# Softmax denominators by three groups a half instead of four, with two accumulating transfers

## The reference

```python
x = x + tanh(g_xattn) * xattn(LN(x), ctx, ctx, 16)      # 16 heads of 32
x = x + tanh(g_ffn) * ffn(LN(x), w_gate, w_up, w_down)  # 512 -> 1536 -> 512

# xattn: rotary q and k, then per head
scores = q @ k.T * scale + slope * (key - query)
attn = softmax(scores, axis=-1)
out = attn @ v

# ffn: 4-bit blockwise weights, 16-bit quantization of x, up, gate, gate * sig, gate * up
```

## Time and profile before

| | |
|---|---|
| median of 3 executions | 1968.52 us (1967.97 to 1970.09) |
| the profiled execution | 1968.86 us, span 1967.1 us |
| PE busy in the span | 1738.3 us (88%) |
| DVE, ACT, POOL busy | 1484.7, 1187.7, 898.7 us |
| a half of the attention | 29.2 to 31.9 us |

### The profile page before, as it was taken

How to read it: one execution, slowest core, us unless ns; L and a number is a source line. 1 busy time by engine, 2 the same in 40 slices (tenths; PEclk the granted TensorE clock), 3 DMA queues, 4 the chain that set the end, 5 groups by cost and what they waited for, 6 DMA issues and landing times. The chain is left out here.

```text
span 1967.1 us, 26173 instructions
## 1 busy us (share of the span) xinstructions
PE 1738.3 (88%) x9360; PEld 662.5 (34%) x9360; DVE 1484.7 (75%) x2117; ACT 1187.7 (60%) x1911; POOL 898.7 (46%) x411
## 2 busy tenths in 40 slices
PE   1899999999999999999986999999999910299999
PEld 0222333323333323333223554544444400044444
DVE  6899888888787787887845665648999999855442
ACT  2476776777777777666651232228997678854441
POOL 3499999989999999998630010110000000000000
PEclk9999999999999999999997999999999965599999
DMA  4332233112332222221024565547885357755542
GB/s 113 88 115 81 77 87 87 48 49 57 87 88 55 59 61 82 76 56 25 20 97 133 179 204 201 185 153 245 261 269 194 131 178 248 236 186 170 177 161 75
DMA packets 170914, 250.45 MB, mean 127 GB/s; under 512 B 30272, under 2 KB 101312, under 8 KB 170272
## 3 DMA queue, kind: packets, MB, share of 16 engines
q1 hardware_dynamic: 170784, 248.78, 40.2%
HBM read 146.74 MB, written 76.68 MB: 114 GB/s over the span
## 5 line engine op out<-in xcount | busy, mean ns | idle before, releaser
L1024 ACT ACTIVATE P<-quad 128x512 f32<-128x512 f32 x1024 | 557.1, 599 | 243.3 <-PE quad L852 242.9
L1205 DVE TENSOR_REDUCE cm<-quad 128x1 f16<-128x1024 f32 x512 | 601.0, 1216 | 116.5 <-PE quad L839 116.3
L1718 POOL TENSOR_TENSOR Ps<-P,P 128x2048 f32<-128x2048 f32 x124 | 563.0, 4540 | 85.5 <-ACT P L1024 85.3
L852 PE MATMUL quad<-QA,KA 101*128 101x512 f16 x1024 | 352.9, 385 | 6.3 <-ACT P L1024 5.2
L984 PE MATMUL quad<-Wd,oh 128*128 128x512 f16 x768 | 231.6, 382 | 129.5 <-DVE ol L1558 129.5
L839 PE MATMUL quad<-KA,QA 100*128 100x512 f16 x1024 | 323.4, 390 | 24.1 <-issue 7.4
L888 PE MATMUL quad<-P,cg 128*32 128x512 f32 x2048 | 272.7, 604 | 3.6 <-ACT numT L1052 0.6
L1098 ACT ACTIVATE ev<-quad 128x1024 f32<-128x1024 f32 x96 | 97.4, 1015 | 209.6 <-PE quad L945 204.9
L1441 DVE TENSOR_REDUCE mxt<-ev 128x1 f32<-128x1024 f32 x96 | 116.8, 1217 | 113.3 <-ACT ev L1098 113.3
L852 PEld LDWEIGHTS quad<-QA,KA 101*128 101x128 f16 x1024 | 84.2, 97 | 344.8 <-ACT P L1024 233.9
L945 PE MATMUL quad<-x_hi,Wg 128*128 128x512 f16 x768 | 189.2, 381 | 3.6 <-DVE x_lo L1437 3.6
(11 more groups left out here) (143 smaller groups left out, 2095.7 us busy)
## 6 DMA issues: line engine op xcount, KB each, us to landing
gate_scratch<-ev SPq DMA_DIRECT2D x48, 512.0 KB, 2.9
gt<-gate_scratch SPq DMA_DIRECT2D x48, 512.0 KB, 5.6
up_scratch<-ev SPq DMA_DIRECT2D x48, 512.0 KB, 3.1
uf<-up_scratch SPq DMA_DIRECT2D x48, 512.0 KB, 4.9
uf<-up_scratch SPq DMA_DIRECT2D x96, 256.0 KB, 3.6
wt_scratch<-wh SPq DMA_DIRECT2D x72, 128.0 KB, 2.6
cg<-in_ctx_dram SPq DMA_DIRECT2D x16, 512.0 KB, 3.8
xl<-in_x_dram SPq DMA_DIRECT2D x32, 256.0 KB, 4.4
```

The lines of the kernel that those rows point to most:

```text
L852: e.matmul(K.score[a], K.KA[k][0:101, a * T + 128 * kt:a * T + 128 * kt + 128], K.QA[k][0:101, T * qc + 512 * a:T * qc + 512 * a + 512], s ...
L1024: e.activation(K.Pb[pb][:, h, :], K.score[h % 2], ACT.Exp, scale=SCALE / (QPOW * KPOW)).then_inc(K.a_exp, 1)
L1205: e.tensor_reduce(cm[:, u:u + 1], K.quad[UNIT["max", hm, u] % 2][:, :], AX.X, ALU.max).then_inc(K.v_max, 1)
L1718: e.tensor_tensor(K.Ps[n % 2][:, :, :], K.Pb[(st.g - 1) % NP][:, :, :], K.Pb[st.g % NP][:, :, :], ALU.add).then_inc(K.g_sum, 1)
```

## The change

The eight key tiles of a half now go into three sums. GpSimd adds tiles 0 and 1 into `Ps0` (s = 1), 3 and 4 into `Ps2` (s = 4), 6 and 7 into `Ps1` (s = 7). Tile 2 is added into `Ps0` and tile 5 into `Ps2` by a transfer each, SBUF to SBUF, which GpSimd issues (s = 3 and s = 6) and which adds to its destination. The groups stand at s = 6 and, of the next half, at s = 1 and 2. The copy of the denominator moves to s = 3, turning and dividing to s = 4, the addition of `x` to s = 5. There is a fifth buffer `P` and a third `Ps`. `exponent` waits for the transfer where a transfer was the last to read the buffer. The tables move the loads, norms, statistics and weight steps by a step or more. The last half stays as it was, with four groups.

```diff
-NXL, NWL, NWQ, NP = 7, 4, 2, 4
+NXL, NWL, NWQ, NP = 7, 4, 2, 5
@@ gate_weight_jobs
-        put(102 + 8 * k, "wround", 0, k)
-        put(103 + 8 * k, "wrounded", 0, k)
-        put(108 + 8 * k, "wscaled", 0, k)
-        put(110 + 8 * k, "wturn", 0, k)
-        put(114 + 8 * k, "wstore", 0, k)
+        put(106 + 8 * k, "wround", 0, k)
+        put(108 + 8 * k, "wrounded", 0, k)
+        put(110 + 8 * k, "wscaled", 0, k)
+        put(115 + 8 * k, "wturn", 0, k)
+        put(118 + 8 * k, "wstore", 0, k)
-NORM_TILES = {9: (0,), 11: (1, 2, 3), 12: (4,), 13: (5, 6), 15: (7,)}
+NORM_TILES = {10: (0, 1), 12: (2, 3, 4), 14: (5, 6), 15: (7,)}
@@ Step
-        self.out = hf - 1 if s == 3 and 1 <= hf <= NHALF else None
+        self.out = hf - 1 if s == (3 if hf == NHALF else 4) and 1 <= hf <= NHALF else None
-        self.add = hf - 1 if s == 4 and 1 <= hf < NHALF else None
+        self.add = hf - 1 if s == 5 and 1 <= hf < NHALF else None
-        self.sum = (hf, s // 2) if self.inside and s % 2 == 1 else None
+        last, inside = hf == NHALF - 1, self.inside and hf < NHALF - 1
+        self.sum = (hf, s // 2) if last and s % 2 == 1 else (hf, {1: 0, 4: 2, 7: 1}[s]) if inside and s % 3 == 1 else None
+        self.accumulate = (hf, s // 6, s - 1) if inside and s in (3, 6) else None
         self.dens = None
-        if s % 2 == 1:
-            h, n = (hf, s // 2 - 1) if s > 1 else (hf - 1, 3)
-            if 0 <= h < NHALF:
-                self.dens = (h, n)
+        if s == 6 and inside:
+            self.dens = (hf, 0)
+        elif s in (1, 2) and 1 <= hf < NHALF:
+            self.dens = (hf - 1, s)
...
-        self.den_out = hf - 1 if s == 2 and 1 <= hf <= NHALF else None
+        self.den_out = hf - 1 if s == (2 if hf == NHALF else 3) and 1 <= hf <= NHALF else None
@@ tensor_program
-                e.wait_ge(K.g_sum, 4 * hf + n + 1)
+                if n == 1:
+                    e.wait_ge(K.g_sum, sum_no(hf, n))
+                else:
+                    e.wait_ge(K.d_acc[n // 2], 16 * hf + 16)
@@ scalar_program, exponent
-            if m // 2 < 4 * (NHALF - 1):
-                e.wait_ge(K.g_sum, m // 2 + 1)
+            hm, km = m // 8, m % 8
+            if hm < NHALF - 1 and km % 3 < 2:
+                e.wait_ge(K.g_sum, 3 * hm + km // 3 + 1)
+            elif hm < NHALF - 1:
+                e.wait_ge(K.d_acc[km // 3], 16 * hm + 16)
@@ gpsimd_program
-            e.tensor_tensor(K.Ps[n % 2][:, :, :], K.Pb[(st.g - 1) % NP][:, :, :], K.Pb[st.g % NP][:, :, :], ALU.add).then_inc(K.g_sum, 1)
+            e.tensor_tensor(K.Ps[n][:, :, :], K.Pb[(st.g - 1) % NP][:, :, :], K.Pb[st.g % NP][:, :, :], ALU.add).then_inc(K.g_sum, 1)
+        if st.accumulate is not None:
+            hf, n, kt = st.accumulate
+            e.wait_ge(K.a_exp, score_no(hf, kt, 3))
+            e.wait_ge(K.g_sum, sum_no(hf, 2 * n))
+            e.dma_start(K.Ps[2 * n][:, :, :], K.Pb[(8 * hf + kt) % NP][:, :, :], accum_op=ALU.add).then_inc(K.d_acc[n], 16)
```

More of the change, by code:

```diff
@@ L142, in __init__ @@
         self.load_context = p + 2 if w == 1 and 1 <= p and p + 2 < NQ else None
-        self.load_columns = p + 3 if w == 5 and 0 <= p and p + 3 < NQ else None
+        self.load_columns = p + 3 if w == 6 and 0 <= p and p + 3 < NQ else None
         self.stack = (p + 1, w - 1) if 0 <= p and 1 <= w <= 4 and p + 1 < NQ else None
         self.rows = self.hm if 0 <= self.hm < NHALF and self.im == 7 else None
-        self.store = p - 1 if w == 6 and 1 <= p <= NQ else None
-        self.sum = (hf, s // 2) if self.inside and s % 2 == 1 else None
+        self.store = p - 1 if w == 7 and 1 <= p <= NQ else None
+        last, inside = hf == NHALF - 1, self.inside and hf < NHALF - 1
+        self.sum = (hf, s // 2) if last and s % 2 == 1 else (hf, {1: 0, 4: 2, 7: 1}[s]) if inside and s % 3 == 1 else None
+        self.accumulate = (hf, s // 6, s - 1) if inside and s in (3, 6) else None
         self.dens = None
-        if s % 2 == 1:
-            h, n = (hf, s // 2 - 1) if s > 1 else (hf - 1, 3)
-            if 0 <= h < NHALF:
-                self.dens = (h, n)
+        if s == 6 and inside:
+            self.dens = (hf, 0)
+        elif s in (1, 2) and 1 <= hf < NHALF:
+            self.dens = (hf - 1, s)
+        elif last and s in (3, 5, 7):
+            self.dens = (hf, s // 2 - 1)
+        elif hf == NHALF and s == 1:
+            self.dens = (hf - 1, 3)
         self.num_out = hf - 1 if s == 1 and 1 <= hf <= NHALF else None
-        self.den_out = hf - 1 if s == 2 and 1 <= hf <= NHALF else None
+        self.den_out = hf - 1 if s == (2 if hf == NHALF else 3) and 1 <= hf <= NHALF else None
         self.stats = None
-        if w >= 13 and 0 <= p < NQ:
-            self.stats = (p, 0, w - 13)
-        elif 5 <= w < 8 and 1 <= p <= NQ:
+        if w >= 14 and 0 <= p < NQ:
+            self.stats = (p, 0, w - 14)
+        elif w == 0 and 1 <= p <= NQ:
+            self.stats = (p - 1, 0, 2)
+        elif p == NQ and 5 <= w < 8:
             self.stats = (p - 1, 1, w - 5)
+        elif 6 <= w < 9 and 1 <= p < NQ:
+            self.stats = (p - 1, 1, w - 6)
         self.aggregate = self.deviation = None
@@ L231, in max_no, with den_no, sum_no @@
     return 16 * hm + u + 1
+def den_no(hf, n):
+    return 3 * hf + n + 1
+def sum_no(hf, n):
+    return 3 * hf + (1, 3, 2)[n]
 def rope_no(p, w):
@@ L333, in __init__ @@
         self.biash = [nc.alloc_sbuf_tensor_at(f"biash{i}", [32, T], F16, offset=at + 4096 + 2048 * i) for i in range(2)]
-        self.Ps = [A(f"Ps{i}", [128, 4, 512], F32) for i in range(2)]
+        self.Ps = [A(f"Ps{i}", [128, 4, 512], F32) for i in range(3)]
         self.numT = A("numT", [128, 512], F32)
@@ L409, in __init__ @@
         self.d_x2s = sem("d_x2s")
+        self.d_acc = [sem(f"d_acc{i}") for i in range(2)]
         self.d_wl = [sem(f"d_wl{i}") for i in range(NWL)]
@@ L912, in tensor_program @@
             else:
-                e.wait_ge(K.g_sum, 4 * hf + n + 1)
+                if n == 1:
+                    e.wait_ge(K.g_sum, sum_no(hf, n))
+                else:
+                    e.wait_ge(K.d_acc[n // 2], 16 * hf + 16)
             for h in range(4):
-                mm = e.matmul(K.den[32 * h:32 * h + 32, :], K.ones[:, :], K.Ps[n % 2][:, h, :], start=n == 0, stop=n == 3)
+                mm = e.matmul(K.den[32 * h:32 * h + 32, :], K.ones[:, :], K.Ps[n % 2 if hf == NHALF - 1 else n][:, h, :], start=n == 0, stop=n == (3 if hf == NHALF - 1 else 2))
             mm.then_inc(K.pe_den, 1)
@@ L1054, in scalar_program @@
             hf = st.den_out
-            e.wait_ge(K.pe_den, 4 * hf + 4)
+            e.wait_ge(K.pe_den, den_no(hf, 3 if hf == NHALF - 1 else 2))
             if hf > 0:
@@ L1376, in vector_program @@
             e.wait_ge(K.a_exp, score_no(st.hf, st.s, 3))
-            e.wait_ge(K.pe_den, 4 * st.hf + n - 1)
+            e.wait_ge(K.pe_den, den_no(st.hf - 1, n) if n < 2 else den_no(st.hf, n - 2))
             e.tensor_tensor(K.Ps[n % 2][:, :, :], K.Pb[(st.g - 1) % NP][:, :, :], K.Pb[st.g % NP][:, :, :], ALU.add).then_inc(K.v_sum, 1)
@@ L1713, in gpsimd_program @@
             hf, n = st.sum
-            k = 4 * hf + n
             e.wait_ge(K.a_exp, score_no(hf, st.s, 3))
-            if k >= 2:
-                e.wait_ge(K.pe_den, k - 1)
-            e.tensor_tensor(K.Ps[n % 2][:, :, :], K.Pb[(st.g - 1) % NP][:, :, :], K.Pb[st.g % NP][:, :, :], ALU.add).then_inc(K.g_sum, 1)
+            if hf > 0:
+                e.wait_ge(K.pe_den, den_no(hf - 1, n))
+            e.tensor_tensor(K.Ps[n][:, :, :], K.Pb[(st.g - 1) % NP][:, :, :], K.Pb[st.g % NP][:, :, :], ALU.add).then_inc(K.g_sum, 1)
[4 more added lines that the diff above has]
+            e.dma_start(K.Ps[2 * n][:, :, :], K.Pb[(8 * hf + kt) % NP][:, :, :], accum_op=ALU.add).then_inc(K.d_acc[n], 16)
     deviation_2(B - 1)
```

## The result

The changed kernel takes 2047.2 us (2043.7 to 2053.4) against 1968.8: a ratio of 1.040, with a 95% interval of 1.0375 to 1.0427. It is 78 us slower, where 20 us faster was forecast. The profiled execution took 2053.4 us.

The account below looks back on a forecast made before the run. TensorE's work was taken as the bound of most halves: -31.3 us for removed groups, +3.0 for VectorE-full halves, +8.4 for VectorE's delay, -19.9 in all, 1948.6 us against the median; range 1938 to 1990.

Parts of the forecast that it names:

- TensorE sets the length of a half; a group costs 0.86 to 1.00 us: Attention halves: one group fewer gives 28.16 us instead of 29.17, 1.01 us a half, 31.3 us over 31 halves.
- VectorE gives back 8.4 us, its full halves 3.0: Delay after the turning, 0.3 us in 28 halves, 8.4 us; no gain in three VectorE-full halves, 3.0 us.
- GpSimd's issues of 1 us each, at no cost: GpSimd in each half: loses one 4.54 us addition, gets two transfer issues of 1 us each, costed at nothing.
- A transfer of 8 us, inside 10: Each 1 MB adding transfer: 4.2 + 2.9 us plus 1 for the issue, about 8, due after 10.0; no cost.
- transfers late: Rival: adding transfers need 11.2 us and land 1.2 us late in each half, 37 us, 1986 us; chance 0.13.
- SP's queue. Nothing is added to it: SP's transfers: the change adds none, and stores of the turned weights leave the place between the stacks; no cost term.
- The sign named ahead of the result: Sign of being wrong: SP's issues grown over 0.62 us, with scores waiting for `QA<-crow`.
- the maxima's row late: Rival: adding transfer holds SP's stack 3.4 us, first score 2.8 us late in 15 quartets, 43 us, 1992; chance 0.12.
- The margin of 1.57 us: First halves of quartets: time the `crow` row has to spare before its score, 0.56 us after the half shortens.
- Another queue need not hold SP's: Argument against the row rival: GpSimd's transfers go in a different queue from SP's stack; no size given.
- a mean DMA share of at most 0.37 over whole halves: Argument against the row rival: DMA share is only 0.00 to 0.37 in the profiled windows.
- engines go round their queues packet by packet: Skill's rule, used against the row rival: the stack would wait for single packets, not for the whole transfer.

Follow-up runs that it names:

- both_short: Changed kernel with both adding transfers of a half cut to a sixteenth, 64 KB each, rest of tiles 2 and 5 left out of the denominators: 1940.0 us, ratio 0.9853.
- second_short: Changed kernel with only the second adding transfer of a half (tile 5 into Ps2) cut to a sixteenth, 64 KB: 1964.8 us, ratio 0.9982.
- experiment 3: Changed kernel with the two transfers of the maxima's row issued from ScalarE's queue instead of by SP behind the stack: 1992.5 us, ratio 1.0114.

## Why the prediction was wrong, point by point

**TensorE sets the length of a half; a group costs 0.86 to 1.00 us.** Right. The changed halves without a late row take 28.27 us, against the sum's 28.16. Over the whole kernel the order is worth 28.5 us by `both_short`.

**VectorE gives back 8.4 us, its full halves 3.0.** Too dark by 8.6 us together: 19.9 forecast, 28.5 measured. From one copy of the numerator to the next, the late halves of `both_short` are 0.90 us shorter than before (28.27 against 29.17), those with weight steps 1.02, the two with row statistics 0.61 and 0.43, and the one with the aggregation is no shorter. So the full halves gave back 2.0 of the 3.0 us, and the 8.4 us of delay hardly occurred: 0.1 us in a late half, none with weight steps.

**GpSimd's issues of 1 us each, at no cost.** Right: 0.86 us, and hidden.

**A transfer of 8 us, inside 10.** Right in the median, 8.0 us, and in its parts: a plain copy took 5.0 where 4.2 + 1 was the term, the addition 3.0 where it was 2.9. The longest took 12.3 us. Nobody waited for the sums to speak of (4.2 us in all). The rival "transfers late" did not occur.

**"SP's queue. Nothing is added to it".** This is the step that failed. Nothing was added to the queue, but its transfers share the engines with the new ones. I priced the transfer for those who wait for its data, and not for those who need the same engines. In its place the runs showed 15 waits for the row, 78.8 us in all, and the slow steps behind them; with the bytes cut to a sixteenth the waits were 1.2 us. The sign named ahead of the result, SP's issues grown over 0.62 us with scores waiting for `QA<-crow`, is what came.

**The rival "the maxima's row late"** had the place and the mechanism, with a chance of 0.12 and 43 us. Its terms were too small. The hold on SP's issues was taken as 3.4 us. It was 3.7 in the stack and 1.0 more in the row's own issue, less the 0.85 that the kernel before had too: the issue ended 29.48 us after the start of the half (956.86 - 927.38) instead of 25.60 (880.87 - 855.27), so 3.9 us later. The landing was taken as 2.0 us from a row without traffic beside it; here the row was issued beside the second transfer, and the score could start 3.9 us after its issue ended. (With no large transfer beside it the row needed less than was taken: in `second_short` most scores start 1.2 us after the issue.) The two make 2.4 us more than the forecast 2.8; the half itself ran 28.26 and not 28.16 us, which takes 0.1 back, and 5.1 was measured. And the slow clock behind the wait, 2.3 us here, was not in it at all: 7.4 us.

**What the time is made of.** The profiled execution took 113.6 us more than that of `both_short` (2053.4 against 1939.8). The waits for the row make 77.6 of it (78.8 - 1.2). The steps that open behind these waits are together 30.1 us longer than the same steps of `both_short`, by the starts of their score matmuls; in 13 of the 15 the first pair of score matmuls takes 1.01 us instead of 0.60. Some 6 us stay open, 2.6 of them in the first half.

**Chances.** The margin of 1.57 us, cut to 0.56 by the gain itself, was in the text. The engines' share of 0.93 in the window from 952.76 could not be known ahead, but 1 MB with two reads against a margin of 0.56 us could, and that was not a case for 0.12. "Another queue need not hold SP's" had no row behind it. The argument against it, a mean DMA share of at most 0.37 over whole halves, was an average over the stretch that mattered, and held none of the new transfers.

The sentence of the Trainium skill (DMA: Bandwidth & Descriptors, Queues, rings and completion order) that engines go round their queues packet by packet was used to make the rival small. The runs do not contradict the rule, but turn after turn did not protect the small transfers: four of SP's issues took 2.5 times as long, and the row landed with the big transfer. A third queue did not protect it either: in experiment 3 the row was in time where it was issued ahead of the big transfer, and late where it was issued behind it. How the engines took their turns no run here shows.

## What to carry to other kernels

Before a large transfer is put beside others, list every small transfer that shares its engines, with the moment it is due. Issue it ahead of the large one, or count on its landing with it. Take the DMA share of the stretch in which the large one is in flight and not the mean. Work taken off the bounding engine also brings every deadline closer, so margins must be read against the shortened step. Where a transfer has room in one half of a loop and not in the other, use it only there.

## What was not expected of the hardware

An adding transfer of 1 MB from SBUF to SBUF lands in 8.0 us and a plain one in 5.0 (6.9 and 4.5 at the least). While one was in flight, four issues of another queue took 1.45 to 1.69 us instead of 0.6. Ten times a small transfer was issued with the adding one in flight and over 2 us to go, and ten times it had landed only within 0.4 us of it; with no large transfer beside it (`second_short`) it was there 1.2 us after the end of its issue.

After a standstill of 5.06 us TensorE's granted clock was 0.59 over the next 6.1 us; after one of 1.26 us it stayed at 1.00. Over all 15 waits of the changed kernel the slow matmuls came behind 13, of 3.4 to 6.8 us; behind the one of 4.06 us only in part, and not behind the one of 1.58 us. With the second transfer cut, 14 of 15 waits were of 0.65 to 2.41 us and had none, and the one of 3.12 us had them. With the row from ScalarE's queue they came behind a wait of 2.36 us, so the length of the wait alone does not decide it.
